# Attention and expert layer on one core: score work in blocks of three weight products instead of couples of two

## The reference

```python
xn = _layernorm(x)
q, k, v = (xn @ W.T).reshape(B, S, 16, 8)    # 16 heads of 8, q and k rotated by rope
scores = einsum('bhqd,bhkd->bhqk', q, k) / sqrt(8)
att = einsum('bhqk,bhkd->bhqd', softmax(scores), v)
h = relu(xn @ up_w[e].T) ** 2                # 32 experts of 64, 6 chosen per row
moe = sum over e of (h * combine[:, e]) @ down_w[e]
shared = relu(xn @ shared_up_w.T) ** 2 @ shared_down_w.T
out = x + att + moe + shared
```

## Time and profile before

| | |
|---|---|
| time, three runs | 613.72, 614.03 (median), 614.72 us |
| profiled execution | 613.97 us, of which the span from first to last instruction is 612.2 us |
| TensorE (PE) busy | 99% of the span, granted clock 1.00 |
| VectorE (DVE), ScalarE (ACT), GpSimd (POOL) busy | 70%, 67%, 70% |
| chain that ended last | PE 91% |

### The profile page before, as it was taken

The page is one execution under the profiler, slowest core; times in us unless marked ns, Lnnn a source line. Parts: engine busy times, 40 slices in busy tenths (PEclk is TensorE's granted clock), DMA queues, the critical chain, the costliest instruction groups (busy, mean ns, idle before and its releaser), DMA issues.

```text
span 612.2 us, 19876 instructions
## 1 busy us (share of the span) xinstructions
PE 603.6 (99%) x8123; PEld 271.1 (44%) x8123; DVE 427.3 (70%) x1058; ACT 407.9 (67%) x803; POOL 427.7 (70%) x512
## 2 busy tenths in 40 slices
PE   8999999999999999999999999999999999999997
PEld 7533544444444444444444434444443443444343
DVE  7898965777757776677867777586766877666402
ACT  3578666667666666766667676676667665666664
POOL 5850477677786778867788678876776766667663
PEclk9999999999999999999999999999999999999999
DMA  5175742746436254653437454263545632343430
GB/s 149 37 239 175 163 114 67 233 106 157 110 73 212 67 156 109 198 144 71 122 84 241 106 155 106 49 226 82 139 112 158 188 77 92 86 105 71 106 71 18
DMA packets 52027, 76.17 MB, mean 124 GB/s; under 512 B 5984, under 2 KB 19168, under 8 KB 51936
## 3 DMA queue, kind: packets, MB, share of 16 engines
q1 hardware_dynamic: 51916, 74.90, 46.0%
q10 hardware_dynamic: 20, 0.00, 0.0%
HBM read 56.14 MB, written 18.35 MB: 122 GB/s over the span
## 4 chain that ended last, share of the span: by engine, by line
PE 91%; DVE 4%; DMA 2%; POOL 1%; issue 1%; SPq 1%; ACT 0%; DVEq 0%; POOLq 0%
PE acc L1060 21%; PE pv L1227 20%; PE st L1060 14%; PE upb L1060 10%; PE st L1197 9%; PE sc L1186 5%; PE upb L1197 4%; PE st L1202 3%; DVE nmax L930 3%; PE upb L1202 1%; PE st L1169 1%; DMA k_stack<-qk_parts 1%; DMA stacks<-k_stack 1%; PE upb L1169 1%; PE st L1152 1%
## 5 line engine op out<-in xcount | busy, mean ns | idle before, releaser
L930 DVE TENSOR_REDUCE nmax<-sc 128x1 f32<-128x512 f32 x512 | 328.6, 686 | 143.7 <-PE sc L1186 132.7
L700 ACT ACTIVATE probs<-st 128x512 f32<-128x512 f32 x359 | 202.8, 595 | 29.1 <-PE st L1202 20.3
L558 POOL TENSOR_TENSOR gated<-gate_at,relu 128x512 f32<-128x512 f32 x111 | 142.0, 1279 | 99.7 <-ACT relu L705 90.4
L562 POOL TENSOR_TENSOR g<-gated,relu 128x512 f32<-128x512 f32 x111 | 142.2, 1281 | 16.2 <-POOL gated L558 0.4
L1202 PE MATMUL st<-stacks 32*128 32x512 f32 x359 | 148.7, 578 | 0.0
L1227 PE MATMUL pv<-probs,v_aug 128*32 128x512 f32 x1024 | 136.4, 605 | 0.1
L1060 PE MATMUL acc<-dn,g 128*32 128x128 f32 x3512 | 135.2, 274 | 1.0 <-issue 1.0
L1186 PE MATMUL sc<-stacks 32*128 32x512 f32 x512 | 132.5, 493 | 1.4 <-DVE nmax L930 1.0
L1060 PEld LDWEIGHTS acc<-dn,g 128*32 128x32 f32 x3512 | 112.2, 114 | 23.9 <-issue 23.8
L700 ACT ACTIVATE probs<-upb 128x512 f32<-128x512 f32 x153 | 91.0, 595 | 21.1 <-PE st L1202 13.6
L1197 PE MATMUL st<-m_rows,ones 3*128 3x512 bf16 x359 | 99.4, 385 | 0.2 <-ACT sh L682 0.2
(11 more groups left out here) (188 smaller groups left out, 569.1 us busy)
## 6 DMA issues: line engine op xcount, KB each, us to landing
gate_at<-gate_rows SPq DMA_DIRECT2D x62, 512.0 KB, 6.6
stacks<-q_stack SPq DMA_DIRECT2D x30, 256.0 KB, 6.7
stacks<-k_stack SPq DMA_DIRECT2D x30, 256.0 KB, 6.8
q_stack<-qk_parts SPq DMA_DIRECT2D x28, 256.0 KB, 6.6
k_stack<-qk_parts SPq DMA_DIRECT2D x28, 256.0 KB, 6.0
x_res<-in_x SPq DMA_DIRECT2D x8, 256.0 KB, 7.3
out<-y SPq DMA_DIRECT2D x8, 256.0 KB, 6.9
m_rows<-m_parts SPq DMA_DIRECT2D x95, 4.0 KB
```

What stands on the lines that cost most here:

```text
L558: nc.gpsimd.tensor_tensor(gated[:, u % 2, :], gate_at[:, group % RING, u % GATES, :], relu[:, u % RELUS, :], ALU.mult).then_inc(gated_read ...
L562: nc.gpsimd.tensor_tensor(g[:, u % 2, :], gated[:, u % 2, :], relu[:, u % RELUS, :], ALU.mult).then_inc(g_ready, 1)
L700: nc.scalar.activation(probs[:, u % 2, h, :], ring_b("st", u * QUAD + h)[:], ACT.Exp).then_inc(probs_ready, 1)
L930: nc.vector.tensor_reduce(out=nmax[:, s % 2, at:at + 1], in_=sc_b[tile % SC_BANKS][:], op=ALU.max, axis=AXX, negate=True).then_inc(s_read, 1)
```

## The change

From unit 16 (batch 1) to unit 123 the couples give way to 144 *blocks* (`triple`), four for each three units. A block holds the maxima and products of three heads in turn (a, b, c) and three score tiles, so that each row tile carries two and a half passes: the head without a product (the spare row tile) gives one whole tile of 512 keys in bank `sc0` and a half of 256 keys; heads a, b, c give a half each. Two halves share a bank: `lone` in `sc1` (the spare's and a's) and `late` in `sc2` (b's and c's), sorted by where their maxima are kept. The two halves of a bank are ordered by a new semaphore, `half_done`.

Of four blocks the second has no unit of its own; the others are followed by `pv`, side work, `expert_up` and half a down, the second by three halves of downs (`downs_at`). With k the block's number, the four kinds are k modulo 4 = 0, 1, 2, 3. VectorE reduces a block's three banks in the order 1, 2, 0 after all three are done (`triple_max`), two maxima per bank, joins the halves of a step by a minimum (`n_joined`, for which `cut_max` now waits), and does the unit's other work behind the reductions. ScalarE does three exponents, the side's copies, then the relu (`triple_out`). The ring of three banks follows the new order. One projection of batch 0 also gets column tiles. SyncE's and GpSimd's instructions keep their order.

```diff
+FIRST_T, LAST_T, PERIOD = SLICES, UNITS - 4, 3
+TRIPLES = (LAST_T - FIRST_T) * QUAD // PERIOD
+HALVES = 2
+FIRST_CUT = 5
...
+def place_triples(scored):
+
+    column = {h: scored // QUAD * HALVES for h in range(QUAD)}
...
+    for k in range(TRIPLES):
+        first = FIRST_T * QUAD + k * PERIOD
+        heads = [i % QUAD for i in range(first, first + PERIOD)]
+        spare, = set(range(QUAD)) - set(heads)
+        own = [take(spare) for _ in range(PERIOD)]
+        if own[0] is None:
+            triples.append((first, None))
+            continue
+        lone = own.pop(0 if own[0][1] % HALVES else -1)
+        triples.append((first, (own[0], [lone, take(heads[0])], [take(heads[2]), take(heads[1])])))
+    assert all(n == TILES * STEPS // QUAD * HALVES for n in column.values())
+    return triples
...
+        def unit_at(k):
+
+            return FIRST_T + k // QUAD * PERIOD + (0, None, 1, 2)[k % QUAD] if k % QUAD != 1 else None
+
+        def downs_at(k):
+
+            u = FIRST_T + k // QUAD * PERIOD
+            return (((u - 2, 0),), ((u - 2, 1), (u - 1, 0), (u - 1, 1)), ((u, 0),), ((u, 1),))[k % QUAD]
...
+            for k, (first, scores) in enumerate(TRIPLE):
+                order += [("st", i) for i in range(first, first + PERIOD)]
+                if unit_at(k):
+                    order += sides(unit_at(k)) + [("up", unit_at(k))]
...
+            def triple_out(k):
+                first = TRIPLE[k][0]
+                for i in range(first, first + PERIOD):
+                    exponent(i // QUAD, i % QUAD)
+                if k == 0:
+                    square_relu(SLICES - 1)
+                u = unit_at(k)
+                if not u:
+                    return
+                side_out(u)
+                relu_out(u)
+                if u % (TT * PAIR) == 0:
+                    att_evac(u // (TT * PAIR) - 1)
...
+            def triple_max(k):
+                dve.wait_ge(s_done, SCORED + (k + 1) * SC_BANKS)
+                dve.wait_ge(n_cut, top_of(k) - 1)
+                places = nmax[:].rearrange("p s e c -> p (s e c)")
+                for bank_at in (1, 2, 0):
+                    low, high = [place_of(half) for half in banks_of(k)[bank_at]]
+                    nc.vector.tensor_reduce(out=places[:, low:high + 1:high - low],
+                                            in_=sc_b[bank_at][:].rearrange("p (e c) -> p e c", e=HALVES),
+                                            op=ALU.max, axis=AXX, negate=True).then_inc(s_read, 1)
+                for s in range(FIRST_CUT, STEPS):
+                    if reads_of(s) == SCORED + (k + 1) * SC_BANKS:
+                        dve.wait_ge(s_read, reads_of(s))
+                        nc.vector.tensor_tensor(nmax[:, s % 2, 0, :], nmax[:, s % 2, 0, :], nmax[:, s % 2, 1, :], ALU.min
+                                                ).then_inc(n_joined, 1)
...
+            for k in range(TRIPLES):
+                if k < SCORE_TRIPLES:
+                    triple_max(k)
+                if unit_at(k):
+                    unit_rest(unit_at(k))
...
+            def half_score(k, bank_at, half, together=1):
+
+                h, n = half
...
+                order = (1, 2, 0).index(bank_at)
+                pe.wait_ge(s_read, SCORED + (k - 1) * SC_BANKS + order + 1 if k else SCORED)
+                to = banks_of(k)[bank_at].index(half) * (T // HALVES)
+                size = together * (T // HALVES)
...
+            def triple(k):
+
+                first, scores = TRIPLE[k]
+                a, b, c = [(i // QUAD, i % QUAD) for i in range(first, first + PERIOD)]
+                weights_max(*a)
+                weights_max(*b)
+                if scores:
+                    whole, lone, late = scores
+                    half_score(k, 1, lone[0]).then_inc(half_done, 1)
+                    half_score(k, 2, late[0]).then_inc(half_done, 1)
+                weights_product(*a)
+                weights_product(*b)
+                if scores:
+                    half_score(k, 0, whole, HALVES).then_inc(s_done, 1)
+                weights_max(*c)
+                weights_product(*c)
+                if scores:
+                    pe.wait_ge(half_done, 2 * k + 1)
+                    half_score(k, 1, lone[1]).then_inc(s_done, 1)
+                    pe.wait_ge(half_done, 2 * k + 2)
+                    half_score(k, 2, late[1]).then_inc(s_done, 1)
...
+            def half_down(u, k, width):
+                b, n = u // SLICES, u % SLICES
+                pe.wait_ge(g_ready, u + 1)
+                if n == 0:
+                    wait(pe, sum_ready, b)
+                m = down_slice(g[:, u % 2, :], dn[:, n, :], n == 0, n == SLICES - 1, width, (range(HT), range(HT, TT))[k])
+                if k:
+                    m.then_inc(down_done, 1)
...
+            for u in range(FIRST_T):
+                unit(u)
+            for k in range(TRIPLES):
+                triple(k)
+                u = unit_at(k)
+                width = P if u and whole(u) else COL
+                if u:
+                    pv(u - 1)
+                    side_work(u)
+                    expert_up(u, width)
+                for e, part in downs_at(k):
+                    half_down(e, part, width)
```

More of the change, by code:

```diff
@@ L97, in place_downs @@
             n -= 1
-place_scores()
+SCORED = place_scores()
+TRIPLE = place_triples(SCORED)
+SCORE_TRIPLES = sum(1 for _, scores in TRIPLE if scores)
 place_downs()
@@ L266, in max_column, with quad_of, place_of, banks_of @@
             return h * TT + qt
+        def quad_of(half):
+            return half[1] // (TT * HALVES)
+        def place_of(half):
+            h, n = half
+            return n // (TT * HALVES) % 2 * (HALVES * TILES) + n % HALVES * TILES + h * TT + n // HALVES % TT
+        def banks_of(k):
+            whole, lone, late = TRIPLE[k][1]
+            h, n = whole
+            return ((h, n), (h, n + 1)), sorted(lone, key=place_of), sorted(late, key=place_of)
+        def top_of(k):
+            return max(quad_of(half) for halves in banks_of(k) for half in halves)
+        def reads_of(s):
+            if (s + 1) * TILES <= SCORED:
+                return (s + 1) * TILES
+            last = max(k for k in range(SCORE_TRIPLES) for halves in banks_of(k) for half in halves if quad_of(half) == s)
+            return SCORED + (last + 1) * SC_BANKS
+        def unit_at(k):
[3 more added lines that the diff above has]
+            return (((u - 2, 0),), ((u - 2, 1), (u - 1, 0), (u - 1, 1)), ((u, 0),), ((u, 1),))[k % QUAD]
         def x_of(i):
@@ L279, in ring_order, with sides @@
         def ring_order():
-            order = []
-            for u in range(UNITS):
+            def sides(u):
                 b, n, kt, q = u // SLICES, u % SLICES, u % TT, u // TT
-                last = u == UNITS - 1
-                order += [("st", u * QUAD), ("st", u * QUAD + 1)]
-                second = [("st", u * QUAD + 2), ("st", u * QUAD + 3)]
-                if last:
-                    order += [("up", u)]
-                if u >= FIRST_LAG:
-                    order += second
+                order = []
                 if kt == ATT_KT and q and q % PAIR == 0:
@@ L310, in ring_order, with couples @@
                         order += [("qk", 2 * (b + 2) + 1)]
-                if u < FIRST_LAG:
-                    order += second
-                if not last:
-                    order += [("up", u)]
+                return order
+            def couples(u):
+                first = [("st", u * QUAD), ("st", u * QUAD + 1)]
+                second = [("st", u * QUAD + 2), ("st", u * QUAD + 3)]
+                if u == UNITS - 1:
+                    return first + [("up", u)] + second + sides(u)
+                return first + (sides(u) + second if u < FIRST_LAG else second + sides(u)) + [("up", u)]
+            order = []
+            for u in range(FIRST_T):
+                order += couples(u)
+            for k, (first, scores) in enumerate(TRIPLE):
+                order += [("st", i) for i in range(first, first + PERIOD)]
+                if unit_at(k):
+                    order += sides(unit_at(k)) + [("up", unit_at(k))]
+            for u in range(LAST_T, UNITS):
+                order += couples(u)
             return order + [("att", STEPS // PAIR - 1)]
@@ L769, in _, with unit_out @@
                     nc.scalar.activation(blank_out[:], blank[:, 0:1], ACT.Exp).then_inc(exp_set, 1)
-            for u in range(UNITS):
+            def unit_out(u):
                 b, n, kt, q = u // SLICES, u % SLICES, u % TT, u // TT
-                if u:
+                if u and u != LAST_T:
                     relu_out(u - 1)
@@ L1048, in _ @@
         def _(pe):
+            FIRST_OF = {}
+            for k in range(SCORE_TRIPLES):
+                whole_half, lone_halves, late_halves = TRIPLE[k][1]
+                for half in (lone_halves[0], late_halves[0], whole_half, lone_halves[1], late_halves[1]):
```

(12 more changed lines are left out.)

92 lines of the change are left out of this document (63 added, 29 removed).

## The result

The changed kernel takes 641.47 us (median of 4 runs, 641.24 to 641.61); the kernel before 613.97 beside it. The ratio is 1.0447, 95% interval 1.0429 to 1.0464: **slower by 27.5 us**, where +31 was predicted. Its profiled execution took 641.59 us with a span of 639.8 at a granted clock of 0.999.

The account below looks back on a forecast made before the run. TensorE, busy 99% of the span, was taken as the bound. 614 us, plus 24.5 for 36 periods of three units, 2 for extra switches and 4.5 at batch ends, gave 645 us; forecast 633 to 657, wider range 616 to 662.

Parts of the forecast that it names:

- Outside the blocks: TensorE's `pv`, up, down and switches between blocks: 8.33 us per three units, 8.55 before; gain only with blocks under 0.88.
- The relu wait: Third maximum waits for the relu of the up product ahead, 0.35 into three blocks of four; block takes 1.02 us.
- The half wait: Second halves wait until first halves are written: alone, blocks of 0.89 us in three kinds, 0.78 in kind 2.
- A block without waits: Two and a half passes on each row tile take 0.67 us if nothing waits.
- the faster case: Rival: blocks take 0.67 to 0.85 us because the waits are covered; 590 to 613 us in all; chance 0.12.
- only part of the waits: Rival: the wait between halves binds alone, or relu or reductions come out shorter; 616 to 632 us; chance 0.14.
- The reduction wait: In kind 2 the whole tile waits for VectorE's reductions until 0.68 into the block, which takes 1.23 us.
- The cold loads: Couples left each unit's next matmul a cold load of some 0.03 us, now only `pv`: 0.09 off per three units.
- The disturbed places: Extra switches of `pv` ahead of transpositions in about 19 units, +2 us; stalls for `add_residual` at batch ends, +4.5 us.
- waits are hidden: Rival: relu, whole tile and halves come early enough, blocks take 0.67 to 0.85 us; 590 to 613 us; chance 0.12.
- Worse: Rival: waits delay the next exponents, reductions and maxima; one more stalled block of four gives 657 to 670 us; chance 0.10.
- In program order: Rival: products wait behind halves on their tiles, blocks about 1.05 us in three kinds, 1.3 in the fourth; about 648; chance 0.08.

Follow-up runs that it names:

- up last: Changed kernel with the up product behind the half down products in each gap, instead of ahead of them: 689.8 us.
- the two runs that moved it: Changed kernel with up behind the half downs, 689.8 us; changed kernel with ScalarE's relu on 128 of 512 tokens, 638.8 us.
- the first two experiments: Changed kernel with up behind the half downs, 689.8 us; changed kernel with block reductions reading a quarter of the keys, 624.0 us.
- the whole tile first: Changed kernel with the whole tile raising its own semaphore and reduced first by VectorE instead of last: 634.8 us.
- both waits taken out: Changed kernel with block reductions reading a quarter of the keys and ScalarE's relu covering a quarter of the tokens: 616.2 us.
- moving another piece in front: Changed kernel with `pv` behind the up product and the half downs dealt out anew over the gaps: 642.3 us.
- the short relu: Changed kernel with ScalarE's relu covering 128 of 512 tokens in the stretch with blocks: 638.8 us.
- short gating: Changed kernel with ScalarE's relu and GpSimd's two gating products covering only 128 of 512 tokens: 628.1 us.

## Why the prediction was right, and where its terms were off

Sign, mechanism and places were right: the waits for the relu and the reductions, which the blocks bring out, cost more than the fewer couples and switches save. That the time came within 3.5 us is luck in part: one term was 13 us too large, and the others together 9 to 10 us too small.

- **Outside the blocks: right.** Predicted 0.89 for `pv`, 0.87 for up, 0.55 for a half down with its switch. Above: 0.88 (301.68 to 302.56), 0.86 (303.42 to 304.28), 0.55 (304.28 to 304.83).
- **The relu wait: right in place and moment, its block mis-sized.** The third maximum was put 0.35 into the block and stands there. The step "the last half stands behind them on the same row tile, 0.12" failed: the last halves are of the block's first two heads, on their tiles, and the first halves are on the spare tile and the third head's. I had read the lists the other way round. So the block ends 0.55 after the third maximum: 0.90, not 1.02, 36 x 3 x 0.12 = 13 us too much.
- **The half wait: mis-sized both ways, to no effect.** Alone it was put at 0.89 in three kinds and 0.78 in the fourth, by the same reading; it measured 0.84 in all, hidden behind the relu as predicted. A block without waits was put at 0.67 and takes at least 0.78, because row tiles were costed as independent: the third maximum would then start 0.12 into the block, and it starts at 0.23, right behind the whole tile. That moved the bounds of the faster case and of "only part of the waits", not the forecast.
- **The reduction wait: right.** Predicted 0.68 into the block and 1.23 long; measured 0.73 and 1.28, since VectorE began 0.23 after the block's end (298.95 to 299.18) and not 0.17. 36 x 0.05 = 2 us too little.
- **The cold loads, -0.09 per period**, do not show: 3 us too little. A typical period is then, from the unrounded medians, 3 x 0.90 + 1.28 = 3.99 of blocks and 3 x (0.88 + 0.86 + 0.55) + 1.45 = 8.33 of gaps, 12.32 against 11.85: +17 us over 36 periods and not +24.5.
- **The disturbed places: too small.** The rest of the stretch, +29.6 - 17 = +12.6 us, was put at 6.5. The five waits for `add_residual` take 1.24, 1.59, 1.24, 1.16 and 1.16 above the usual (6.4, predicted 4.5 at four batch ends); `pv` ahead of the 25 places where attention, gates or x are turned takes 3.9 more (predicted 2 for about 19), 1.3 of it in three places that wait as well; and the blocks above their kind's median add 4.3 that were not predicted. The longest (2.28 at 242.1, 2.03 at 470.9) follow VectorE's held instructions (shown above for the first; 1.27 and 1.33 us from 467.90 on for the second); others (1.54 at 154.7 and 384.3, 1.67 at 535.0) wait for a bank that VectorE's attention output (L1065) still reads. Together 14.6, of which the pieces before had 2.2 as well.
- **Ahead of the stretch** 0.1 was predicted and 2.0 gained, cause open.

Sum: 17 + 12.6 - 2 = 27.6, against 27.5.

One sign of the prediction did not come: TensorE's waits of L1197's successor, L1338, for about 100 relus. In the stretch with blocks the view of waits names one (0.2 us), and with up last 89. The view names a wait only where the engine stood idle, and 0.35 into a block other matmuls still run. The wait shows in the 0.65 us from relu to maximum and in the two runs that moved it.

Of the rivals, "waits are hidden" fell with the first two experiments. "Worse" is there in small: the 4.3 us of long blocks are its mechanism. "In program order" came near in time for a wrong reason: it had the products behind halves on their tiles and a block of 1.05, and without their waits the blocks take 0.84 in the median. Inside the blocks the starts do stand in program order (298.06 to 298.51, and so in all 140 blocks with scores), and a wait for a semaphore holds what follows it on other tiles (the whole tile first). In the kernel before the starts do not, and the earlier trace rows are not the only place: in 225 of the 242 couples with scores the two scores start ahead of both products, which stand ahead of them in program order, as here (0.03 us):

```profile
303.29 0.50 PE L1186 MATMUL sc<-stacks 32*128 32x512 f32 x2
303.32 0.58 PE L1202 MATMUL st<-stacks 32*128 32x512 f32 x2
```

The Trainium skill says ("TensorE: Matmul & The Clock Gate", Part 3) that matmuls start in program order. The blocks agree with it, the couples do not, and no run took up what makes the difference.

The break-even of 0.88 us per block tells why nothing saved the change: even 0.84, with both waits taken out, is worth 36 x 4 x 0.04 = 6 us, and the disturbed places cost 12.

## What to carry to other kernels

Fewer, denser blocks on a bound engine remove the slack that other engines lived in: for each bank that a block takes, work out from rows when its last reader starts, add the reader-to-reuse time (0.65 us here after a relu's start, 2.2 after a block's end for three reductions), and compare it with what now stands between. Read from the lists themselves which tile each piece is on before charging a queue. When a wait is covered by moving another piece in front, ask what that piece was covering where it stood, since here all 17 us came back.

## What was not expected of the hardware

Small VectorE instructions on SBUF (128x32, 0.2 us) take 1.0 to 1.35 us where they meet a GpSimd product of 1.28 us: with the short relu, the 13 long ones of the routing's lines 977 to 988 in units 16 to 123 all end 0.05 to 0.09 us after such a product. Most have two inputs in SBUF; L1021 above, with one, took 1.20. The Trainium skill ("SBUF — State Buffer", "SBUF: two separate sides") says that the two engines take a shared port pair for a whole instruction, the other one blocked; the rows agree. The score reductions, which read PSUM, keep their 0.6 us. So an edit that only moves GpSimd's start can lengthen VectorE's work: 12 held instructions before, 22 after the change, 34 with a shorter relu, 13 with the whole tile reduced first, none with short gating. It does not always cost time: with relu and reductions both short 44 were held, and no block after the first took more than 0.85.
